# Edge counting in a graph network kernel: one packed register per stretch, one eviction per stretch, chores in another order

## The reference, cut to what matters

```python
h = relu(layernorm(x));  x = x + relu(mean_dst(h[src]) @ Wl.T + b + h @ Wr.T)     # L0
h = relu(layernorm(x));  x = x + sage(relu(sage(h)))                              # L1A, L1B, means by dst
h = relu(layernorm(x));  x = x + layernorm(h + relu(h @ Ws.T + b + mean_src((h @ Wn.T + bn)[dst]))) * g + be   # L2
h = relu(layernorm(x));  x = x + gcn(relu(gcn(h)))                                # L3A, L3B, sums by dst, scaled by degree
```

## Time and profile before

| | us |
|---|---|
| median of three executions | 723.08 |
| the profiled execution | 723.23 |
| its span, first to last instruction | 721.5 |
| counting stage, until the first aggregation (L1217) | 188.3 |
| PE busy in the span | 671.5 (93%) |
| DVE, ACT busy | 408.4 (57%), 286.8 (40%) |

### The profile page before, as it was taken

The page is one execution under the profiler, slowest core; times in us unless marked ns, Lnnn a source line. Parts: engine busy times, 40 slices in busy tenths (PEclk is TensorE's granted clock), DMA queues, the critical chain, the costliest instruction groups (busy, mean ns, idle before and its releaser), DMA issues.

```text
span 721.5 us, 11380 instructions
## 1 busy us (share of the span) xinstructions
PE 671.5 (93%) x3199; PEld 526.2 (73%) x3200; DVE 408.4 (57%) x951; ACT 286.8 (40%) x525; POOL 18.3 (3%) x26
## 2 busy tenths in 40 slices
PE   4948888889899999999999999999999899999997
PEld 3325565666688888888888888888877678887786
DVE  6977776666357544332443466655799871247333
ACT  2656565576343222465212342212444352223321
POOL 2000000000000000000000000000322000000000
PEclk9979999999899999999999999999999999999999
DMA  7101211011402000210000210000200000000011
GB/s 248 48 1 25 72 31 22 18 36 36 106 0 73 1 0 0 76 58 1 0 0 0 75 58 1 0 0 1 75 0 1 0 2 1 0 1 0 31 59 55
DMA packets 22801, 21.94 MB, mean 30 GB/s; under 512 B 13676, under 2 KB 13988, under 8 KB 22760
## 3 DMA queue, kind: packets, MB, share of 16 engines
q1 hardware_dynamic: 21480, 18.85, 9.2%
q10 hardware_dynamic: 1280, 2.56, 1.0%
HBM read 15.57 MB, written 2.56 MB: 25 GB/s over the span
## 4 chain that ended last, share of the span: by engine, by line
PE 81%; issue 5%; DVE 5%; ACT 3%; ACTq 2%; DVEq 2%; DMA 1%; SPq 0%
PE ps L1217 35%; PE ps L1140 33%; PE ps L1112 8%; PE ps L1133 3%; ACTq L240 1%; DMA wstage<-in_L_gnn_W_l 1%; DVEq L240 1%; ACT cstage L480 1%; PE ps L1092 1%; DVE src_hot L717 1%; ACT count L428 1%; DVE own L948 1%; ACT apart L446 1%; PE ps L1080 0%; DVE stats L695 0%
## 5 line engine op out<-in xcount | busy, mean ns | idle before, releaser
L1217 PE MATMUL ps<-p_hi,cstage 128*128 128x512 f32 x600 | 236.2, 394 | 6.4 <-issue 4.6
L1217 PE MATMUL ps<-p_lo,cstage 128*128 128x512 f32 x600 | 235.0, 392 | 0.0
L1140 PE MATMUL ps<-w_hi,hT_hi 128*128 128x512 f32 x400 | 162.4, 406 | 2.1 <-DVE hT_lo L756 2.0
L1140 PE MATMUL ps<-w_hi,hT_lo 128*128 128x512 f32 x400 | 156.6, 391 | 0.0
L1140 PE MATMUL ps<-w_lo,hT_hi 128*128 128x512 f32 x400 | 156.0, 390 | 0.0
L1217 PEld LDWEIGHTS ps<-p_hi,cstage 128*128 128x128 f32 x600 | 113.6, 189 | 31.9 <-issue 8.4
L1217 PEld LDWEIGHTS ps<-p_lo,cstage 128*128 128x128 f32 x600 | 113.6, 189 | 23.3
L920 DVE SCALAR_TENSOR_TENSOR own<-ps,nodal,own 128x512 f32 (+1 forms) x60 | 44.9, 749 | 124.6 <-PE ps L1217 124.2
L480 ACT CAST cstage<-countT 128x1280 fp32r (+1 forms) x50 | 62.6, 1262 | 90.9 <-PE ps L1217 90.0
L1112 PE MATMUL ps<-src_hot,dst_hot 128*128 128x320 bf16 x420 | 76.2, 330 | 22.0 <-ACT dst_hot L450 14.4
L717 DVE TENSOR_SCALAR src_hot<-iota,nodeT 128x640 bf16<-128x640 f16 x210 | 74.5, 381 | 25.5 <-PE ps L1112 13.1
(11 more groups left out here) (130 smaller groups left out, 477.8 us busy)
## 6 DMA issues: line engine op xcount, KB each, us to landing
x<-in_x ACTq DMA_DIRECT2D x1, 2304.0 KB
out_x<-x SPq DMA_DIRECT2D x9, 256.0 KB
wstage<-in_L_gnn_W SPq DMA_DIRECT2D x2, 1024.0 KB, 5.2
wstage<-in_L_gnn_W_l SPq DMA_DIRECT2D x1, 1024.0 KB, 8.8
w_own<-in_L_gnn_W_r SPq DMA_DIRECT2D x1, 1024.0 KB, 9.4
vec<-in_L_gnn_b SPq DMA_DIRECT2D x4, 256.0 KB, 5.5
wstage<-in_L_gnn_W1l SPq DMA_DIRECT2D x1, 1024.0 KB, 5.6
wstage<-in_L_gnn_W1r SPq DMA_DIRECT2D x1, 1024.0 KB, 5.4
```

Of the source, the lines that this page charges most:

```text
L1140: last = nc.tensor.matmul(ps[:, bank, :], a[:, r, k, :], w[:, slot, k, :], start=n == 0, stop=n == len(pairs) - 1)
L1217: last = nc.tensor.matmul(ps[:, AGG + r, :], cstage[:, part, k, :], p_[:, k, :], start=n == 1, stop=n == 2 * len(parts) * NT)
```

## The change

Four things change together.

1. Registers. The table becomes one number per stretch, `256 * tiles + first tile` (`tiles_of`). Each engine reads it at each stretch (one value, 20 times per engine, PE too), splits it by `& 255` and `>> 8`, and keeps its own running count of visits in a register. The small chain that builds the table is shorter (19 steps to 13), two casts in it move to ACT.
2. Evicting. A stretch is copied in one ACT instruction of 128 partitions, as it lies in PSUM: partitions 64 to 127 hold the counts of sources above 640. Putting in order is left to the DMA: 20 transposes of five tiles instead of ten of ten, a `countT16` in another layout that `stage` reads in runs of 64, and, for the one layer (L2) that aggregates by source, an exchange of two quarters of `count16` through DRAM (`swap`). The degrees come out by window and are put in order by four small DVE copies.
3. The split of the one-hots. ACT makes `dst_hot` for four tiles of six (BY_ACT = 4) and DVE for two.
4. Order. The first weight comes in two halves, issued before the wait for the edges, and x is asked for once they have landed; its transposes stand around the table. Block 1 is written out with block 0. In a block ACT now evicts each stretch before it begins the next one; PE does `turn` between the stretches; DVE does `lo`, `statistics`, `p_rest` in that order after the second stretch.

```diff
-    HALF = RING // 2
+    BY_ACT = 4
-    countT16, _ = place("countT16", [P, NT, NP], U16)
+    countT16, _ = place("countT16", [P, NW, NT, WIN], U16)
...
-    def visits_of(engine, b, blocks):
-        _, found = nc.values_load_multi_w_load_instructions(
-            for_hots[0:1, bass.ds(2 * b, 2 * blocks), 0:3], engines=[engine.engine], bass_reorder=False)
...
+    def visits_of(engine, visited, b, h):
+        _, (packed,) = nc.values_load_multi_w_load_instructions(
+            tiles_of[0:1, window(b, h)], engines=[engine.engine], bass_reorder=False)
+        t0, length = engine.snap(packed & 255), engine.snap(packed >> 8)
+        n0 = engine.snap(visited, min_val=0, max_val=NW * (ETP + RING))
+        offset = engine.snap(t0 - n0)
+        n1 = nc.s_assert_within(engine.snap(n0 + length), RING, NW * (ETP + RING),
+                                skip_runtime_bounds_check_because=IN_TABLE)
+        engine.reg_mov(visited, n1)
+        return n0, n1, offset
...
-            order = [("f", 0), ("v", rows[0]), ("f", 1), ("v", rows[1]), ("t", 0), ("t", 1), loads[0]]
+            order = [("f", 0), ("f", 1), ("f", 2), ("v", rows[0]), ("v", rows[1]), ("t", 0), ("t", 1), loads[0]]
...
-                    sp.dma_start_transpose(countT16[:, :, what * P:(what + 1) * P], count16[:, what, :]
-                                           ).then_inc(cT_loaded, 16)
+                    for h in range(2):
+                        sp.wait_ge(counts_out, 2 * what + h + 3)
+                        sp.dma_start_transpose(
+                            countT16[:, 2 * what + h, :, :].rearrange("p (c q) d -> p c (q d)", q=2),
+                            count16[:, what, h * NS:(h + 1) * NS]).then_inc(cT_loaded, 16)
+                elif kind == "s":
+                    wait_turned_counts(sp)
+                    parts = [(WIN * q, NS * (1 - q)) for q in range(2)]
+                    for k, (a, f) in enumerate(parts):
+                        sp.dma_start(swap[k], count16[a:a + WIN, :, f:f + NS]).then_inc(swap_out, 16)
+                    sp.wait_ge(swap_out, 32)
+                    for k, (a, f) in enumerate(parts):
+                        sp.dma_start(count16[a:a + WIN, :, f:f + NS], swap[1 - k]).then_inc(swapped, 16)
...
-            act.wait_ge(src_loaded, 32 + 16 * bool(REST))
+            for k, loaded in enumerate((dst_loaded, src_loaded)):
+                act.wait_ge(loaded, 16 * (2 + bool(REST)))
+                nc.scalar.copy(e_f[:, k, :, :], e_int[:, k, :, :]).then_inc(cast_done, 1)
+            act.wait_ge(first_loaded[1], 16)
             act.wait_ge(x_pad_set, 1)
             dma_rows(act, x_dram, x, x_loaded)
...
-                for q in range(2):
-                    nc.scalar.activation(
-                        count16[WIN * h:WIN * h + WIN, bass.ds(b, 1), q * NS:(q + 1) * NS].rearrange(
-                            "p o (a n) -> p (o a) n", a=2),
-                        ps[WIN * q:WIN * q + WIN, COUNT + 2 * h:COUNT + 2 * h + 2, 0:NS // 2],
-                        ACT.Copy, accum_out=deg_parts[WIN * h:WIN * h + WIN, q, bass.ds(b, 1)]).then_inc(counts_out, 1)
+                nc.scalar.activation(count16[:, bass.ds(b, 1), h * NS:(h + 1) * NS].rearrange("p o (a n) -> p (o a) n", a=2),
+                                     ps[:, COUNT + 2 * h:COUNT + 2 * h + 2, 0:NS // 2], ACT.Copy,
+                                     accum_out=deg_win[:, bass.ds(b, 1), h]).then_inc(counts_out, 1)
...
             def merged(b, r):                                  # vector
-                givers(b, 0, *first)
-                if owned:
-                    first_own(b - 2)
-                features(L0, b, r)
-                givers(b, 1, *second)
-                p_rest(L0, b - 1, 1 - r)
+                givers(b, 0)
+                features(L0, b, r)
+                first_own(b - 2)
+                givers(b, 1)
+                lo(L0, b, r)
+                if not (isinstance(b, int) and b == NT - 1):
+                    statistics(0, b + 1)
+                p_rest(L0, b - 1, 1 - r)
```

336 lines of the change are left out of this document (176 added, 160 removed).

## The result

| | us, median | range, runs |
|---|---|---|
| before | 723.00 | 722.85 to 723.21, 4 |
| changed | 705.12 | 705.09 to 706.36, 4 |

The ratio is 0.9757, 95% interval 0.974 to 0.9774. The profiled execution took 705.11 us, its span is 703.3. Forecast were 716.4 us, with a range that began at 707: the sign was right, the gain of 6.7 us should have been 18.

What follows compares the result with a forecast made beforehand. PE was taken to be busy from 188.3 us on, and held up by register reads and a lower clock in counting. Gains 2.8 + 5.2 - 1.75 + 0.36 + 0.1 = 6.7 us gave 716.4, range 707 to 727.

Steps and rivals of the forecast that it cites:

- What bounds the kernel: Counting stage: PE waits 1.7 to 2.7 us before blocks behind ACT's or DVE's register reads; long waits lower the clock.
- the waits of 1.75 us per block: Counting blocks: PE stalls of 1.4 us before a block and 0.35 inside it, added to a clean block.
- Part 1, the registers: Counting stretches: one-value reads replace reads of 2.7 us, costing 0.7 us uncovered, 0.4 beside an eviction, nothing on PE.
- Part 4, the order: Counting blocks: ACT's chain of 4.3 us against PE's 2.95 across block ends, 3.7 against 3.3 inside; no clock charge.
- The clean block: Counting stage: a one-group block without waits takes 10.15 us, as block 8 did; two groups 13.75.
- Part 3, four tiles of six: Counting groups: ACT's fourth tile adds 0.4 us per chain and 0.35 before a second group; DVE loses 8.7 busy.
- Part 2, the single eviction: Counting stretches: one ACT eviction of 0.8 us replaces two of 0.8; ends 0.8 and 1.6.
- The start: Before block 2: both weight halves at about 8.7 us, block 2 starting 0.1 us earlier, ends 4 either way.
- the sum of 720: Start, by the skill's DMA rule: halves land late, ACT's chain starts 3.6 us later, total about 720 us.
- A (PE-bound): Counting stage: reads hide, ACT is as quick as before, blocks 1 to 9 run clean; 698 us, chance 0.06.
- my middle case: Counting stage: the read hidden and the stall halved; 708 to 712 us, chance 0.16.
- B's falls of the clock: Blocks 2 to 9: a stall of 2.0 us lowers the clock, 1.4 us more per block; 732 us, chance 0.18.

Runs made afterwards that it cites:

- e6: Kernel before, with only ACT's and DVE's reads changed to one packed value per stretch, mask instead of checks: 709.3 us.
- e11: Changed kernel with the mask, each stretch evicted in two instructions of 64 partitions instead of one of 128: 721.7 us.
- e15: Changed kernel with the mask, old orders from block 2, three of six tiles on ACT, deviation moved behind the first stretch's receivers: 704.7 us.
- e7: Changed kernel with the mask, ACT and DVE reading three values per stretch (two unused), without checks: 717.9 us.
- e17: Like e15 (old orders, deviation later), but ACT makes two of six receiver tiles and DVE four: 709.0 us.
- e10: Changed kernel with the mask, three of six receiver tiles on ACT instead of four: 708.5 us.
- e13: Changed kernel with the mask, old orders on ACT, DVE and PE from block 2, four of six tiles still on ACT: 708.3 us.
- e8: Changed kernel with the mask, first weight asked for only after the edges landed and x at once, as before: 712.7 us.
- e5: Changed kernel, number of visits masked by & 127, one more register operation per read, no check: 710.0 us.
- e12: Changed kernel with the mask and 64 more register moves on PE between counting and the first aggregation: 709.6 us.
- e3: Changed kernel with bounds checks on reads, ACT and DVE reading three values per stretch (two unused): 735.5 us.

## Why the prediction was wrong

**What bounds the kernel: right, and the cause too.** "What holds ACT or DVE is a register read": e6 shows that taking these reads away gives as much as the whole change. That the granted clock would be 1.00 over blocks 2 to 8, and that PE would wait for `dst_hot` of ACT, was right as well.

**The step that failed: the waits of 1.75 us per block that the sum adds to a clean block.** I had 96.2 us for blocks 2 to 8, and 90.57 were measured. The 5.6 between are made up of these: the waits at the blocks' starts, 9.8 us forecast (7 x 1.4) and 6.9 measured; those in the middle, 2.45 (7 x 0.35) and 0.3; those in front of a second group, 2.1 (6 x 0.35) and 3.4 (6 x 0.57), the one term that I had too low; and the rest, 81.85 and 80.0. Of the other 5.9 us of the miss 3.6 are the start, 1.0 block 9 with the tail and 1.3 the layers.

**Part 1, the registers: mis-sized where an eviction runs meanwhile.** I charged 0.7 us uncovered and 0.4 covered. The trace has 0.48 to 0.62 across a block's end, and in its middle 0.13 to 0.23, once 0.41. The read with what belongs to it takes 0.9 us of the sequencer, and it runs beside the instruction ahead of it: an eviction covers nearly all of it. The end of 0 that I gave (wholly hidden) was close, and I took 0.4 without a row for it. In the middle this alone ends the stall of 0.35.

**Part 4, the order: right in kind.** ACT's chain of 4.3 us across a block's end is 4.2 in the trace (127.06, the closing matmul, to 131.28, the next ring group). PE has 3.1 us to do meanwhile (until 130.17), not 2.95. The wait is 1.06 to 1.11 in front of the blocks 6 to 9 and 0.82 to 0.96 in front of the blocks 2 to 5, where I had 1.35 rounded up to 1.4. That ACT's chain is what counts, e11 and e15 show by dose, and e7 with both engines dearer: 0.39 per stretch for 0.43 (e7), 0.50 to 0.64 for 0.8 (e11), 0.31 per block for 0.29 (e15). That DVE "hides behind ACT" was right for the changed kernel, by all 20 ring groups of blocks 2 to 8; in e15 and e17, with ACT's chain shorter, DVE's pace shows.

**The clean block: 9.9 us, not 10.15.** Block 8 before had no wait in front of its ring, but I took that for clean. Its first ring group took 2.05 us at DVE's pace, where 1.80 is full pace. Without its wait of 1.08 block 8 now takes 9.84, and the blocks 5 to 7 take 9.9 each; over seven blocks that is the 1.8 us of the last of the four terms.

**Part 3, four tiles of six: sized about right, and not asked whether it pays.** I took 0.35 us in front of the second group and 0.4 in each chain. The wait in front of a second group is 0.57 with four tiles and 0.17 or none with three (e10), so 0.4 or a little more for the fourth tile. e10 and e13 show that in blocks 2 to 8 the split costs 1.8 to 3.7 us, more than it spares DVE.

**Part 2, the single eviction: right.** For 128 partitions 0.70 + 0.20 (0.79 with their overlap), against my 0.8, as for 64 (e11).

**The start: mis-sized, 3.6 us.** I had the halves at 8.7 us, where 8.3 is measured, and gave most of the gain back to a wait for `lo` (1.6 us; it is 1.25) and a longer chain of ACT in front of block 2. Block 2 started at 61.34. With the old order of the loads (e8) it starts at 64.67, much as in the kernels with packed reads alone (64.29 and 64.33), so most of the start's gain is the loads, as far as single traces tell. The start also scatters: e5 and e12 have the same code there and 62.49 and 60.54, with falls of the clock at other places, so that the 2.7 us between the medians of e8 and e5 are the firmer figure. What of the rest is scatter and what my chain in front of block 2, I cannot tell. The advice of the Trainium skill that I had weighed (page "DMA: Bandwidth & Descriptors", section "Rules for kernel authors": DMAs of 1 MiB or more, issue early and wait late) spoke against this part; the rows disagree with the sum of 720 that I had worked out by it. Two halves of 512 KB, with no x beside them, landed in 4.2 us; with x asked for at the same time, in 8.7 (e8). By that sum they would have been there at 12.3; they were there by 8.3. Whether one whole DMA, with no x beside it, would do as well or better, and what x asked for late is worth by itself, no run here shows.

**Block 9, the tail and the layers: 1.0 and 1.3 us.** PE is busy 1.2 us less in the layers, at a clock of 1.00 against 0.99. I had said that a difference of over 1 us there means that I missed something. 1.03 us of it lie in the first aggregation, ahead of the next transposes (188.31 to 231.77 before, 171.44 to 213.87 now), where the granted clock is 0.96 on the mean instead of 0.94. No experiment isolates it.

**The rivals.** A (PE-bound) named the direction of the miss, and my middle case between it and the forecast, 708 to 712 at 0.16, was nearest. Its condition, the read hidden and the stall smaller, is half of what happened: the read is hidden in the middle of a block, and the waits of 1.75 became 1.0 there. I had priced the terms I was unsure of high: the covered read at 0.4 where its range went down to 0, and the start at 0.1 with 4 to either side. B's falls of the clock near 2 us are there (e3, e11), but not behind every such wait, and the margin to them is larger than I said.
